# A stack of four graph layers on one Trainium2 core: the additive layer's layer norm and elu additions made by VectorE instead of GpSimd

## The chip, the cores and the metric

One Trainium2 chip, one of its cores. The metric is the device time of one execution in microseconds. A core has TensorE (PE, matrix products), VectorE (DVE), ScalarE (ACT), GpSimd (POOL) and SyncE (SP, which here only issues DMAs). They run side by side and wait for each other through semaphores.

## The reference

The input x holds 8 graphs of 1024 nodes with 64 features, adj one 1024x1024 mask per graph. Four layers follow one another, each after a layer norm with a relu, each added to x:

```python
h = jnp.maximum(_layernorm(x, axis=-1), 0.0)
x = x + _L0_gnn_ref(h, adj, ...)      # dot-product attention, one head
h = jnp.maximum(_layernorm(x, axis=-1), 0.0)
x = x + _L1_gnn_ref(h, adj, ...)      # dot-product attention, four heads
h = jnp.maximum(_layernorm(x, axis=-1), 0.0)
x = x + _L2_gnn_ref(h, adj, ...)      # additive attention: the layer of this change
h = jnp.maximum(_layernorm(x, axis=-1), 0.0)
x = x + _L3_gnn_ref(h, adj, ...)      # graph attention with a norm of its own
```

with

```python
def _layernorm(x, axis=-1, eps=1e-05):
    m = jnp.mean(x, axis=axis, keepdims=True)
    v = jnp.var(x, axis=axis, keepdims=True)
    return (x - m) / jnp.sqrt(v + eps)

def _L2_gnn_ref(h, adj, lin_w, lin_b, W_w, a):
    hp = jnp.einsum('bni,oi->bno', h, lin_w) + lin_b
    u = jnp.einsum('bnf,of->bno', hp, W1)
    v = jnp.einsum('bnf,of->bno', hp, W2)
    s = u[:, :, None, :] + v[:, None, :, :]
    s = jnp.where(s > 0, s, ALPHA * s)
    e = jnp.einsum('bijf,f->bij', s, a[:, 0])
    e = jnp.where(adj > 0, e, NEG_INF)
    attention = jax.nn.softmax(e, axis=2)
    h_prime = jnp.einsum('bij,bjf->bif', attention, hp)
    return jax.nn.elu(h_prime)
```

The costly part of the additive layer is s: for each graph 1024 x 1024 pairs of nodes by 64 features, each with its own kink before the sum over features.

## The kernel before, in words

x stays in SBUF for the whole program, as 128 partitions x 8 graphs x 8 blocks x 64 features. Each layer is a block of its own with one program per engine. The additive layer starts at some 1390 us of the span and ends at some 3380 us.

**Units.** The layer goes through 8 graphs (b) and, in each, 8 units (n) of 128 rows: 64 units. A unit's scores are the sum of 16 sets (positions k = 0 to 15). A set is 8 rows of the unit times 1024 columns, in four groups. Each set is made by one of two engines and summed by PE into a PSUM bank pair, one for even and one for odd units:
- DVE makes its sets in `make_set` (L1089), two instructions of 128x2048 f32 per set, called ring pieces below. They go to a ring of 4 sets, and DVE waits only if the set four back has not been summed.
- ACT makes 6 or 7 of the 16 sets of a unit (`SCALAR_SETS`, 7 in units 1 and 5), four instructions of 128x1024 per set (L975), into a ring of 3.
- PE takes the sets in the order of k, whoever made them (`sum_set`, L912 for ACT's and L922 for DVE's).

**What else stands in a unit.** Everything else is put at a fixed position k by hand. For the unit before: the masked maximum on DVE at k = 3 (L257, then negmax at L260), the exponential on ACT at 6 (L269), the turning of the rows on PE at 7 (L198), the two copies out of PSUM at 10 (L239, half on DVE and half on ACT), the product with the values on PE at 11 (L220), the division on DVE at 15 (L1143, L1145). For the next graph: nine fills, which are the small products that make its inputs. PE makes three in each of units 1, 2 and 3 at k = 3, 7 and 11, and DVE takes each out of PSUM three positions later (`take_fill`; L1008 takes fills 0 and 1, L1010 fills 2 and 3). The coding of the next graph's inputs into half-precision parts is on DVE in units 4 to 7 (L1025 to L1079). The last graph has no fills and no coding.

**The layer norm.** It is worked two graphs ahead, graph b making the normed rows of graph b + 2 (the last two graphs make those of graphs 0 and 1 for the next layer). DVE makes the mean in unit 4 at k = 4 (`layer_norm_mean`, L137 and L139). POOL then subtracts it and squares (`layer_norm_centre`, L148 and L151). DVE sums the squares and makes the variance in unit 6 at k = 6 (`layer_norm_scale`, L168 and L156). POOL then makes the inverse root (`inverse_root`, L161, on 8 numbers per partition) and multiplies by it (`layer_norm_apply`, L179). These POOL operations, but for the root, are 128x512 f32.

**The elu.** When a graph is done, in unit 1 of the next one, DVE makes min(z, 0) and max(z, 0) - 1 at k = 1 (`elu_parts`, L766 and L767), ACT makes the exponential of the former at its k = 4 (L773), and POOL adds the two (L874) and adds the sum to x (L876). After the last graph the same is done once more, with nothing beside it, and then the block ends and the next layer starts (its first DVE instruction is L1529).

Semaphores of the change: `mean_ready`, `square_ready`, `seed_ready` (the variance), `y_ready` (the normed rows), `elu_exp`, and `x_added`, which counts two per graph. DVE itself waits for `x_added` before it uses the elu's two tiles for coding (unit 5) and before the next `elu_parts`. PE waits for `y_ready` before the fills that turn the normed rows, `fill_ready` says that it has, and that tile may be overwritten.

Of the kernel before, what the change touches and what calls it, by code (L numbers as in the profile page):

```python
# [36 lines left out]
ALU = mybir.AluOpType  # L37
# [3 lines left out]
P = 128  # L41
# [9 lines left out]
STARTS = 1  # L51
# [3 lines left out]
def wait(eng, sem, value):  # L55

    if not isinstance(value, int) or value > 0:
        eng.wait_ge(sem, value)
# [67 lines left out]
def next_norm(s, b):  # L126

    return b + 2 - s.B if isinstance(b, int) and b + 2 >= s.B else b + 2
# [4 lines left out]
def layer_norm_mean(v, s, sems, b, done):  # L133

    nc = s.nc
    wait(v, sems["y_ready"], done)
    nc.vector.tensor_reduce(s.stat[:, 0, :], s.graph(b), AX.X, ALU.add)  # L137
    v.drain()
    nc.vector.tensor_scalar(s.stat[:, 1, :], s.stat[:, 0, :], 1.0 / s.D, None, ALU.mult).then_inc(sems["mean_ready"], 1)  # L139


def layer_norm_centre(g, s, sems, b, done):

    nc = s.nc
    shape = [P, s.NB, s.D]
    g.wait_ge(sems["mean_ready"], done + 1)
    wait(g, sems["y_ready"], done)
    nc.gpsimd.tensor_tensor(s.centred[:], s.graph(b), s.stat[:, 1, :].unsqueeze(2).to_broadcast(shape),  # L148
                            ALU.subtract).then_inc(sems["centred_ready"], 1)
    g.wait_ge(sems["centred_ready"], done + 1)  # L150
    nc.gpsimd.tensor_tensor(s.square[:], s.centred[:], s.centred[:], ALU.mult).then_inc(sems["square_ready"], 1)  # L151


def variance(v, s, stat, total):

    return s.nc.vector.tensor_scalar(stat[:, 3, :], total, 1.0 / s.D, LN_EPS, ALU.mult, ALU.add)  # L156


def inverse_root(g, s, stat, out):

    return s.nc.gpsimd.tensor_tensor(out, stat[:, 3, :], s.minus_half[:], ALU.pow)  # L161


def layer_norm_scale(v, s, sems, b, done):

    nc = s.nc
    v.wait_ge(sems["square_ready"], done + 1)
    nc.vector.tensor_reduce(s.stat[:, 2, :], s.square[:], AX.X, ALU.add)  # L168
    v.drain()
    variance(v, s, s.stat, s.stat[:, 2, :]).then_inc(sems["seed_ready"], 1)  # L170


def layer_norm_apply(g, s, sems, b, par, done, y_free):

    g.wait_ge(sems["seed_ready"], done + 1)
    inverse_root(g, s, s.stat, s.stat[:, 7, :])
    g.drain()
    wait(g, sems["fill_ready"], y_free)
    s.nc.gpsimd.tensor_tensor(s.y[:, par, :, :], s.centred[:],  # L179
                              s.stat[:, 7, :].unsqueeze(2).to_broadcast([P, s.NB, s.D]),  # L180
                              ALU.mult).then_inc(sems["y_ready"], 1)
# [596 lines left out]
def additive_layer(nc, s, lin_w, lin_b, W_w, a_w):  # L778
# [5 lines left out]
    B, N, D, NB = s.B, s.N, s.D, s.NB  # L784
    K = 9
# [6 lines left out]
    with ExitStack() as ctx:  # L792
        def sb(name, shape, dt):
            return ctx.enter_context(nc.sbuf_tensor(f"l2_{name}", shape, dt))

        sems = make_sems(nc, ctx, "l2", ["vector_sets", "scalar_sets", "vector_summed", "scalar_summed", "coded", "elu_parts", "elu_exp",
                                         "raw_turned", "x_added"])
        raw = sb("raw", [D, 3, D], F32)
        lwT = sb("lwT", [P, D], F32)
        w1 = sb("w1", [P, 2, D], F32)  # L800
# [17 lines left out]
        low, high = (s.mask[:, 2 + i, :].bitcast(F32).rearrange("p (j d) -> p j d", j=NB) for i in range(2))  # L818
# [49 lines left out]

        @block.gpsimd
        def _(g):  # L870
            def elu_add(b):

                g.wait_ge(sems["elu_exp"], b + 1)
                nc.gpsimd.tensor_tensor(high[:], high[:], low[:], ALU.add).then_inc(sems["x_added"], 1)  # L874
                g.wait_ge(sems["x_added"], STARTS + 2 * b + 1)
                nc.gpsimd.tensor_tensor(s.graph(b), s.graph(b), high[:], ALU.add).then_inc(sems["x_added"], 1)  # L876

            for b in range(B):
                layer_norm_centre(g, s, sems, next_norm(s, b), b + 2)
                layer_norm_apply(g, s, sems, next_norm(s, b), b % 2, b + 2, b * K + 2)  # L880
                elu_add(b)

        @block.tensor
        def _(pe):
# [117 lines left out]
        def _(v):  # L1002
# [91 lines left out]
            def run(b, par, n, u, buf, fills, before=True, encode=False):  # L1094
                first, count = fills
                for k in range(SETS):
                    if k not in ON_SCALAR[n]:
                        make_set(par, n, u, k)
                    if k in TAKE_AT and TAKE_AT[k] < count:
                        take_fill(b + 1, 1 - par, first + TAKE_AT[k])  # L1100
                    if n == 4 and k == 4:
                        layer_norm_mean(v, s, sems, next_norm(s, b), b + 2)
                    if n == 6 and k == 6:
                        layer_norm_scale(v, s, sems, next_norm(s, b), b + 2)
                    if encode and n == 4 and k in (7, 11):
                        extremes(0, k // 11, w[:, 1 - par, :])
                    if encode and n == 5 and k in (2, 4):
                        extremes(1, k // 4, r[:, 1 - par, :])
                    if encode and n == 5 and k == 7:
                        find_range(1 - par)  # L1110
                        wait(v, sems["x_added"], STARTS + 2 * b)
                    if encode and (n, k) in ((5, 11), (6, 11)):
                        code_half_w(1 - par, n - 5)
                    if encode and n == 7 and k == 4:
                        code_r(1 - par)
                    if encode and n == 7 and k == 11:
                        code_signs(1 - par)
                    if k == BATCH and n == 1 and b > 0:
                        batch_end(b - 1)
                    if not before:  # L1120
                        continue
                    if k == MAX:
                        logit(1 - buf, u - 1)
                    if k == COPY:
                        copy_half(v, nc.vector.tensor_copy, s, sems, 0, u - 1)
                    if k == FINISH:
                        finish((n - 1) % NB, 1 - buf, u - 1)

            def batch_end(b):
                v.drain()  # L1130
                wait(v, sems["x_added"], STARTS + 2 * b)
                elu_parts(v, s, sems, z[:], low, high)
# [8 lines left out]
            def finish(n, slot, u):  # L1141
                v.wait_ge(sems["out_ready"], u + 1)
                nc.vector.reciprocal(s.rinv[:, slot:slot + 1], unit_out[:, D:D + 1])  # L1143
                v.drain()
                nc.vector.tensor_scalar(z[:, bass.ds(n, 1), :].rearrange("p a d -> p (a d)"), unit_out[:, 0:D],  # L1145
                                        s.rinv[:, slot:slot + 1], None, ALU.mult).then_inc(sems["unit_done"], 1)
# [52 lines left out]
            copy_half(v, nc.vector.tensor_copy, s, sems, 0, u)  # L1199
            finish(NB - 1, 1, u)  # L1200
            batch_end(B - 1)

# [406 lines left out]
```

## Time and profile before

| | |
|---|---|
| median of 3 runs | 3784.64 us (3781.56 to 3786.26) |
| the profiled execution, its own time | 3785.15 us |
| span of the profiled execution | 3783.4 us |
| mean granted TensorE clock | 0.954 of full speed |
| busy, share of the span | PE 84%, DVE 86%, ACT 78%, POOL 27% |

Busy time of an engine is the time in which one of its instructions runs; waiting, semaphore and DMA-issuing instructions are left out. Instructions of one engine overlap a little, so a start-to-start step can be shorter than the duration shown. A line number is the line of the kernel, and where a helper makes an instruction, the helper's. The timeline merges neighbouring instructions of one kind: x4 means four of them, and the time is from the first's start to the last's end. In brackets stands the idle time of the engine before the row and what ended it.

### The profile page before, as it was taken

What the parts mean: (1) busy time and instruction counts of PE and PEld (TensorE: products, weight loads), DVE (VectorE), ACT (ScalarE), POOL (GpSimd) and SP (SyncE); (2) the same over time, 40 slices, a digit from 0 to 9 for tenths busy, and PEclk for the clock granted to TensorE, in tenths of its full rate; (3) what the DMA queues carried; (4) which work ended last, traced back from release to release, by engine and by line L of the source; (5) the groups of instructions that cost most, each with busy time, mean ns of one, the idle gap of its engine ahead of it and who ended that gap; (6) DMA issues with size and microseconds to landing.
All of it is one profiled execution on the core that took longest, in us unless ns stands there. A gap on an engine that the chain in (4) does not pass through costs nothing. (4 is left out here: it accounts for less than half of the span.)

```text
span 3783.4 us, 80082 instructions
## 1 busy us (share of the span) xinstructions
PE 3194.2 (84%) x31515; PEld 1745.3 (46%) x31515; DVE 3269.9 (86%) x5325; ACT 2960.2 (78%) x3529; POOL 1014.7 (27%) x565
## 2 busy tenths in 40 slices
PE   6886988998999878889898898888988978878786
PEld 4663666665666643333333333333333323336665
DVE  7885887887888779999999999999999999966666
ACT  4554877887788758989899899888998889956555
POOL 4332555555555630000000001000000000016554
PEclk9997999999999989999999999999999999988887
DMA  6551000000000000000000000000000000001111
GB/s 180 172 183 38 18 17 17 18 18 19 18 18 15 21 13 7 10 12 10 10 10 10 10 10 10 10 10 10 11 12 10 10 10 10 10 14 52 49 51 43
DMA packets 67260, 110.69 MB, mean 29 GB/s; under 512 B 25941, under 2 KB 25944, under 8 KB 66904
## 3 DMA queue, kind: packets, MB, share of 16 engines
q1 hardware_dynamic: 66904, 105.77, 9.4%
q8 instruction: 245, 4.01, 0.4%
q14 instruction: 111, 0.91, 0.1%
HBM read 86.87 MB, written 18.87 MB: 28 GB/s over the span
## 5 line engine op out<-in xcount | busy, mean ns | idle before, releaser
L975 ACT ACTIVATE l_scalar_ring<-l_w,l_r 128x1024 f32<-128x1024 f32 x1600 | 1679.8, 1143 | 35.7 <-DVE l_values L1021 26.1
L1089 DVE TENSOR_SCALAR l_vector_ring<-l_w_code,l_r_code 128x2048 f32<-128x2048 f32 x1248 | 1619.2, 1362 | 3.5 <-issue 0.2
L922 PE MATMUL scores<-l_vector_ring,l_signs_code 128*32 128x512 f16 x9984 | 686.4, 396 | 194.8 <-DVE l_vector_ring L1089 193.7
L912 PE MATMUL scores<-l_scalar_ring,l_signs 128*32 128x512 f32 x6400 | 781.3, 607 | 67.7 <-ACT l_scalar_ring L975 66.7
L239 ACT COPY probs_t<-turned 128x512 f32<-128x512 f32 x512 | 293.4, 586 | 494.7 <-PE turned L198 491.5
L434 POOL TENSOR_TENSOR l_masked<-l_relu,mask 128x1024 f32<-128x1024 f32 x256 | 545.5, 2131 | 493.8 <-ACT l_relu L582 491.2
L922 PEld LDWEIGHTS scores<-l_vector_ring,l_signs_code 128*32 128x32 bf16 x9984 | 240.0, 96 | 669.8 <-DVE l_vector_ring L1089 399.2
L209 PE MATMUL outT<-probs_t,l_values 128*64 128x128 f32 x6144 | 436.6, 285 | 66.0 <-ACT probs_t L239 26.3
L198 PE MATMUL turned<-ident,l_probs 128*128 128x128 f32 x3072 | 437.7, 288 | 11.4 <-issue 7.3
L209 PEld LDWEIGHTS outT<-probs_t,l_values 128*64 128x64 f32 x6144 | 345.1, 140 | 214.6 <-DVE l_acc L665 102.4
L269 ACT ACTIVATE l_probs<-l_logits,negmax,l_bound 128x1024 f32<-128x1024 f32 x320 | 397.6, 1242 | 6.8 <-DVE negmax L260 6.8
L912 PEld LDWEIGHTS scores<-l_scalar_ring,l_signs 128*32 128x32 f32 x6400 | 197.1, 111 | 442.8 <-issue 265.7
L257 DVE CUSTOM_DVE_ANT_0 l_logits<-scores,l_masked 128x1024 f32<-128x1024 f32 x256 | 313.4, 1224 | 98.5 <-POOL l_masked L434 62.8
L198 PEld LDWEIGHTS turned<-ident,l_probs 128*128 128x128 f32 x3072 | 348.4, 146 | 83.1 <-issue 69.9
L239 DVE COPY probs_t<-turned 128x512 f32<-128x512 f32 x384 | 263.4, 686 | 56.4 <-PE turned L198 51.8
L148 POOL TENSOR_TENSOR centred<-x_res,stat 128x512 f32<-128x512 f32 x32 | 41.5, 1298 | 889.7 <-DVE stat L139 889.5
L582 ACT ACTIVATE l_relu<-scores 128x1024 f32<-128x1024 f32 x256 | 260.2, 1016 | 6.5 <-PE scores L509 6.5
L508 PE MATMUL scores<-l_kh,l_q 128*128 128x512 f16 x640 | 246.6, 385 | 12.4 <-ACT l_values L567 5.0
L509 PE MATMUL scores<-l_kl,l_q 128*128 128x512 f16 x640 | 247.2, 386 | 0.0
L161 POOL TENSOR_TENSOR stat<-stat,minus_half 128x8 f32<-128x8 f32 x32 | 70.3, 2197 | 492.5 <-DVE stat L156 491.9
L231 PE MATMUL outT<-add_halves,turned_out 128*128 128x64 f32 x640 | 127.2, 280 | 81.1 <-DVE turned_out L246 80.5
L1290 POOL TENSOR_TENSOR l_base<-l_dst_slope,mask 128x1024 f32<-128x1024 f32 x64 | 144.2, 2257 | 120.7 <-DVE negmax L260 100.9
(244 smaller groups left out, 3331.8 us busy)
## 6 DMA issues: line engine op xcount, KB each, us to landing
mask<-masks_kept SPq DMA_DIRECT2D x192, 256.0 KB, 2.6
l_adj<-adj SPq DMA_DIRECT2D x64, 512.0 KB, 4.4
masks_kept<-mask SPq DMA_DIRECT2D x64, 256.0 KB, 2.3
x_res<-x SPq DMA_DIRECT2D x8, 256.0 KB, 5.0
out<-x_res SPq DMA_DIRECT2D x8, 256.0 KB, 3.5
l_w_both<-L_gnn_Wq SPq DMA_DIRECT2D x2, 64.0 KB
l_w_both<-L_gnn_Wk SPq DMA_DIRECT2D x2, 64.0 KB
l_w_both<-L_gnn_Wv SPq DMA_DIRECT2D x2, 64.0 KB
```

The lines of the kernel that those rows point to most:

```text
L198: last = s.nc.tensor.transpose(s.turned[:, j, :], probs[:, j * P:(j + 1) * P], s.ident[:])
L209: last = s.nc.tensor.matmul(s.outT[half * s.D:(half + 1) * s.D, 0:P], values[:, j, :], s.probs_t[:, j, :], start=(j < 2), stop=(j >= s.NB ...
L239: copy(s.probs_t[:, half * n:(half + 1) * n, :], s.turned[:, half * n:(half + 1) * n, :]).then_inc(sems[f"half{half}_copied"], 1)
L257: s.nc.vector.tensor_tensor_reduce(out=out, in0=logits, in1=mask, scale=1.0, scalar=-3e38, op0=ALU.add, op1=ALU.max, accum_out=s.rowmax[:, ...
L269: s.nc.scalar.activation(probs, logits, ACT.Exp, bias=s.negmax[:, slot:slot + 1], scale=scale, accum_out=total).then_inc(sems["probs_ready ...
L434: nc.gpsimd.tensor_tensor(masked[:, n % 2, :], relu4[:, n % 2, :], s.mask[:, i, :], ALU.add).then_inc(sems["masked_ready"], 1)
L509: last = nc.tensor.matmul(out, lhs, kl[:, par, h, cols], start=False, stop=True)
L582: nc.scalar.activation(relu4[:, n % 2, :], scores[n % 2], ACT.Relu, scale=1.0 / SLOPE - 1.0).then_inc(sems["relu_ready"], 1)
L912: last = nc.tensor.matmul(s.scores[g * ROWS:(g + 1) * ROWS, buf, half, :], signs[:, window], scalar_ring[:, at % SCALAR_RING, g, halves[ha ...
L922: last = nc.tensor.matmul(s.scores[g * ROWS:(g + 1) * ROWS, buf, half, :], signs_code[:, par, g % 2, window], parts(vector_ring[:, at % VE ...
L975: last = nc.scalar.activation(scalar_ring[:, at % SCALAR_RING, g, :], w[:, par, :], ACT.Relu, bias=r[:, par, column:column + 1])
L1089: last = nc.vector.tensor_scalar(vector_ring[:, at % VECTOR_RING, g:g + 2, :], w_code[:, par, :, :], r_code[:, par, 0, column:column + 1], ...
```

## The change

VectorE gets the five tensor-tensor operations per graph, and GpSimd keeps the inverse root. The centring and square are put in unit 4 at k = 9, the scaling in unit 6 at k = 14, and the elu's additions in unit 1 at k = 8, and after the last graph. Between two operations of one pair there is now a drain on DVE in place of a semaphore. The scaling waits for a new semaphore, `root_ready`.

```diff
         @block.gpsimd
         def _(g):
-            def elu_add(b):
-
-                g.wait_ge(sems["elu_exp"], b + 1)
-                nc.gpsimd.tensor_tensor(high[:], high[:], low[:], ALU.add).then_inc(sems["x_added"], 1)
-                g.wait_ge(sems["x_added"], STARTS + 2 * b + 1)
-                nc.gpsimd.tensor_tensor(s.graph(b), s.graph(b), high[:], ALU.add).then_inc(sems["x_added"], 1)
-
             for b in range(B):
-                layer_norm_centre(g, s, sems, next_norm(s, b), b + 2)
-                layer_norm_apply(g, s, sems, next_norm(s, b), b % 2, b + 2, b * K + 2)
-                elu_add(b)
+                g.wait_ge(sems["seed_ready"], b + 3)
+                inverse_root(g, s, s.stat, s.stat[:, 7, :]).then_inc(sems["root_ready"], 1)
...
                     if n == 4 and k == 4:
                         layer_norm_mean(v, s, sems, next_norm(s, b), b + 2)
+                    if n == 4 and k == 9:
+                        centre_rows(next_norm(s, b), b + 2)
                     if n == 6 and k == 6:
                         layer_norm_scale(v, s, sems, next_norm(s, b), b + 2)
+                    if n == 6 and k == 14:
+                        scale_rows(b, par)
+                    if n == 1 and k == 8 and b > 0:
+                        elu_add(b - 1)
...
+            def centre_rows(g, done):
+
+                shape = [P, NB, D]
+                v.wait_ge(sems["mean_ready"], done + 1)
+                nc.vector.tensor_tensor(s.centred[:], s.graph(g), s.stat[:, 1, :].unsqueeze(2).to_broadcast(shape), ALU.subtract)
+                v.drain()
+                nc.vector.tensor_tensor(s.square[:], s.centred[:], s.centred[:], ALU.mult).then_inc(sems["square_ready"], 1)
+
+            def scale_rows(b, par):
+
+                v.wait_ge(sems["root_ready"], b + 1)
+                v.wait_ge(sems["fill_ready"], b * K + 2)
+                nc.vector.tensor_tensor(s.y[:, par, :, :], s.centred[:], s.stat[:, 7, :].unsqueeze(2).to_broadcast([P, NB, D]),
+                                        ALU.mult).then_inc(sems["y_ready"], 1)
+
+            def elu_add(b):
+
+                v.wait_ge(sems["elu_exp"], b + 1)
+                nc.vector.tensor_tensor(high, high, low, ALU.add)
+                v.drain()
+                nc.vector.tensor_tensor(s.graph(b), s.graph(b), high, ALU.add).then_inc(sems["x_added"], 2)
...
             finish(NB - 1, 1, u)
             batch_end(B - 1)
+            elu_add(B - 1)
```

## Rows read from the trace of the kernel before

**Rows 1.** The page's busy times of the whole span: engine, us, share, instructions.

```profile
PE 3194.2 (84%) x31515; PEld 1745.3 (46%) x31515; DVE 3269.9 (86%) x5325; ACT 2960.2 (78%) x3529; POOL 1014.7 (27%) x565
```

**Rows 2.** Window: us; PE, PEld, DVE, ACT, POOL busy; clock; DMA share; GB/s.

```profile
1423.00:3363.00 1940.00, 1677.17 (x18432) 665.07 (x18436) 1894.30 (x1980) 1759.10 (x1721) 101.33 (x46) 0.98 0.03 10
```

**Rows 3.** Waits of DVE in that stretch: us in total, times, longest.

```profile
DVE l_hpT L1010 <- PE fill L893: 13.6, 7, 2.1
```

**Rows 4.** The ring pieces' line: duration in ns, least/median/most, first and last start.

```profile
L1089 DVE TENSOR_SCALAR l_vector_ring<-l_w_code,l_r_code x1248: 1325/1340/2379, 1423.2 to 3361.7; 128x2048 f32<-128x2048 f32 x179
...
L1089 DVE TENSOR_SCALAR l_vector_ring<-l_w_code,l_r_code 128x2048 f32<-128x2048 f32 x1248 | 1619.2, 1362 | 3.5 <-issue 0.2
```

**Rows 5.** Timeline of POOL in one graph: start, us, instruction, idle before.

```profile
2101.79 3.73 POOL L161 TENSOR_TENSOR stat<-stat,minus_half 128x8 f32<-128x8 f32 x1 [61.24 <-DVE stat L156]
2105.66 1.97 POOL L179 TENSOR_TENSOR y<-centred,stat 128x512 f32<-128x512 f32 x1
2186.73 1.29 POOL L874 TENSOR_TENSOR mask<-mask 128x512 f32<-128x512 f32 x1 [79.10 <-ACT mask L773]
2188.10 2.14 POOL L876 TENSOR_TENSOR x_res<-x_res,mask 128x512 f32<-128x512 f32 x1
2281.15 2.07 POOL L148 TENSOR_TENSOR centred<-x_res,stat 128x512 f32<-128x512 f32 x1 [90.90 <-DVE stat L139]
```

**Rows 6.** Timeline of DVE: ring pieces over those, undisturbed, and a graph later.

```profile
2101.62 8.35 DVE L1089 TENSOR_SCALAR l_vector_ring<-l_w_code,l_r_code 128x2048 f32<-128x2048 f32 x6
...
2106.65 2.07 DVE L1089 TENSOR_SCALAR l_vector_ring<-l_w_code,l_r_code 128x2048 f32<-128x2048 f32 x1
...
2187.34 6.50 DVE L1089 TENSOR_SCALAR l_vector_ring<-l_w_code,l_r_code 128x2048 f32<-128x2048 f32 x4
...
2194.36 5.10 DVE L1089 TENSOR_SCALAR l_vector_ring<-l_w_code,l_r_code 128x2048 f32<-128x2048 f32 x4
...
2280.98 6.56 DVE L1089 TENSOR_SCALAR l_vector_ring<-l_w_code,l_r_code 128x2048 f32<-128x2048 f32 x4
...
2432.36 7.03 DVE L1089 TENSOR_SCALAR l_vector_ring<-l_w_code,l_r_code 128x2048 f32<-128x2048 f32 x4
```

**Rows 7.** DVE tensor-tensor work in the last layer: one line's durations, and a timeline.

```profile
L1490 DVE TENSOR_TENSOR l_work<-l_work,l_gamma x8: 681/940/2240, 3489.1 to 3778.1; 128x512 f32<-128x512 f32 x8
...
3557.96 0.68 DVE L1473 TENSOR_TENSOR l_work<-l_high,l_low 128x512 f32<-128x512 f32 x1
3558.71 0.69 DVE L1475 TENSOR_REDUCE l_total<-l_work 128x8 f32<-128x512 f32 x1
```

**Rows 8.** Timelines of PE and DVE in unit 1, up to the fill.

```profile
2196.08 1.92 PE L912 MATMUL scores<-l_scalar_ring,l_signs 128*32 128x512 f32 x16 [0.96 <-ACT l_scalar_ring L975]
...
2198.95 1.09 PE L198 MATMUL turned<-ident,l_logits 128*128 128x128 f32 x8
...
2199.39 0.67 DVE L1008 TENSOR_SCALAR hT<-fill 64x512 f32<-64x512 f32 x1
...
2207.85 0.68 DVE L1010 COPY l_hpT<-fill 64x512 f32<-64x512 f32 x1 [2.05 <-PE fill L893]
```

**Rows 9.** Unit 1 a graph later: PE, DVE; a window (columns of rows 2).

```profile
2436.93 1.81 PE L922 MATMUL scores<-l_vector_ring,l_signs_code 128*32 128x512 f16 x16 [1.85 <-DVE l_vector_ring L1089]
...
2446.09 0.69 DVE L239 COPY probs_t<-turned 128x512 f32<-128x512 f32 x1 [0.34 <-PE turned L198]
...
2437.00:2441.00 4.00, 4.00 (x32) 1.27 (x36) 4.00 (x4) 4.00 (x5) 0.00 (x0) 0.57 0.00 0
```

**Rows 10.** Timelines of the last graph (unit 5) and of the layer's end.

```profile
3297.63 0.69 DVE L239 COPY probs_t<-turned 128x512 f32<-128x512 f32 x1 [4.21 <-PE turned L198]
...
3376.14 0.63 ACT L773 ACTIVATE mask<-mask 128x512 f32<-128x512 f32 x1 [5.65 <-DVE mask L767]
...
3378.18 1.26 POOL L876 TENSOR_TENSOR x_res<-x_res,mask 128x512 f32<-128x512 f32 x1
...
3379.83 0.11 DVE L1529 MEMSET l_w<- 64x64 f32 x1 [3.73 <-PEq L792]
```

More of the change, by code:

```diff
@@ L796, in additive_layer @@
         sems = make_sems(nc, ctx, "l2", ["vector_sets", "scalar_sets", "vector_summed", "scalar_summed", "coded", "elu_parts", "elu_exp",
-                                         "raw_turned", "x_added"])
+                                         "raw_turned", "x_added", "root_ready"])
         raw = sb("raw", [D, 3, D], F32)
```

## The prediction, made before the changed kernel was run

> **What bounds the kernel now.** I read the page first: VectorE (DVE) is busy for 86% of the span, TensorE (PE) for 84%, ScalarE (ACT) for 78%, GpSimd (POOL) for 27% [rows 1]. That is an average over four layers, and the change touches one, so I cut out its main stretch by windows, from the first to the last piece that DVE makes for the ring: 1940 us in which DVE is busy for 1894 us (98%), ACT for 91%, PE for 86% and POOL for 5% [rows 2]. The waits of DVE in that stretch hold only one regular item, 2.05 us once per graph, 13.6 us in seven waits [rows 3]. So each microsecond of DVE work is a microsecond of the layer, except where DVE stands just before such a wait.
>
> Next, what POOL's work does to DVE. The main instruction, the ring piece at L1089, took 1340 ns at the median, 1362 ns in the mean and 2379 ns at most over 1248 pieces [rows 4]: some of them are stretched. The timelines of POOL and DVE side by side show which. In one graph POOL makes six instructions, of which [rows 5] hold five; the square comes right behind the centring. An undisturbed run of four ring pieces takes 5.10 us. The four pieces that lie over POOL's centring and square take 6.56, which is 1.46 more. The six over the root and the scaling take 8.35, where six undisturbed ones would take 5.10 + 2 x 1.255 = 7.61, which is 0.74 more. The four over the two additions of the elu take 6.50, which is 1.40 more, and one graph later 7.03, 1.93 more [rows 6]. POOL loses too: its second addition took 2.14 us there and 1.26 us at the layer's end, where DVE does nothing [rows 5, 10]. The root by itself (3.73 us on POOL) stretches nothing: the extra 0.74 lies in the one piece of 2.07 us that begins at 2106.65, under the scaling [rows 6].
>
> A rule of the Trainium skill is stricter than these rows. Its page "SBUF — State Buffer", section "SBUF: two separate sides", says that the port pair shared by VectorE and GpSimd is an exclusive lock, held for a whole instruction, while the other engine fully blocks. The rows show 0.7 us of delay per POOL tensor operation, less than the 1.26 us that an addition takes undisturbed, so in my sum the rows decide; what the rule would make of it is rival C.
>
> **The change, part by part.**
> Taken away: five POOL tensor operations per graph, and with them the stretch of DVE's pieces. Over the layer that is 8 x 1.46 = 11.7 us for centring and square, 8 x 0.74 = 5.9 us for the scaling, and for the elu (seven times inside the loop, three times at about 1.4 and four at about 1.9) 11.8 us. Together 29.4 us. As a check, the mean less the median over all pieces gives 0.022 x 1248 = 27.5 us [rows 4].
> Added: five tensor-tensor operations of 128x512 f32 on DVE per graph. The same form with two plain SBUF inputs took 0.68 us at L1473 [rows 7]. Started back to back, instructions cost about 0.08 us less than their duration (four of 1.34 in 5.10), so 0.60 us; with a drain behind it the step from one start to the next is 0.75 us [rows 7]. Centring and square: 0.75 + 0.60 = 1.35 us. Scaling: 0.60. Two additions: 1.35. No trace row has a DVE operation with an input repeated along the row. I bound it from below by 0.68 us (L1473) and from above by the longest of L1490, which has one repeated along the other axis: 681 ns least, 940 median, 2240 most [rows 7]. I take 0.68, since the least of L1490 equals it and its long ones lie beside POOL's work of the last layer.
> Not on the path: the new waits. DVE reaches position 14 of unit 6 eight positions after it gave POOL the variance. Five of these are its own sets of two pieces, so at least 5 x 2 x 1.255 = 12.5 us pass, while the root takes 3.73 us; if the root were late by x, all ring pieces behind it would be late by x. ACT's exponential of the elu is done at its position 4, DVE asks for it at position 8. The mean is DVE's own. No DMA is moved, and POOL's queue holds nothing else that anyone waits for.
>
> Now what of each pair reaches the end.
> *Centring and square* (unit 4): 1.46 - 1.35 = 0.11 us gained per graph, in a DVE-bound stretch. Seven graphs: 0.8 us. In the eighth, DVE waits 4.21 us for the turned rows one unit later [rows 10], which swallows it.
> *Scaling* (unit 6): 0.74 - 0.60 = 0.14 us, eight graphs, 1.1 us.
> *Elu* (unit 1): on DVE's own account 11.8 - 7 x 1.35 = 2.4 us. But here ACT sets the pace: PE waited 0.96 us for an ACT piece just before it turned the rows, DVE ended the piece of work ahead of the copy at 2200.06, the turn was done at 2200.04, and DVE then waited 2.05 us for the fill behind the next ACT piece [rows 8]. A shorter DVE path makes that wait longer. What can come back is a side effect in the later graphs: the stretched piece starves PE for 1.85 us, the granted clock of the four microseconds behind is 0.57 (part of it at 1.2 instead of 2.4 GHz), and both DVE and ACT then wait 0.35 us for the turned rows [rows 9]. With no such stretch this goes: 3 graphs x 0.35 = 1.0 us (the fourth, the last graph, has its 4.21 us wait behind it).
> *The layer's end*: ACT's exponential ends at 3376.77; POOL's additions end at 3379.44 and the next layer starts at 3379.83 [rows 10]. On DVE the two end 0.75 + 0.68 us after the exponential, at 3378.2: 1.2 us gained, with nothing to hide it.
>
> **Sum:** 0.8 + 1.1 + 1.0 + 1.2 = 4.1 us less. The profiled execution took 3785.15 us (3783.4 of span and 1.75 around it), so 3781.0; the median of the three runs is 0.5 below the profiled one, so I forecast **3780.5 us**, 0.11% less. About 0.2% (7.6 us) is what a measurement of this kernel can tell from no change, so this counts as the same.
>
> **Rivals.**
> A. *DVE's account counts everywhere.* If ACT's hold on unit 1 gives way when DVE's path shortens, all of it counts: 29.4 removed, 8 x 1.35 + 8 x 0.60 + 7 x 1.35 = 25.1 added, 1.2 at the end: 5.5 us less, 3779.1. For it: DVE is busy 98%. Against: the 2.05 us wait. Still the same within 0.2%. Chance 0.14.
> B. *Slower: the tensor-tensor operations cost DVE much more than 0.68 us.* Place: units 4 and 6, where DVE has no wait to cover them, 8 x 3 operations. At 1.3 us, between the median and the longest of L1490 [rows 7], each costs 0.62 more: 14.9 - 4.1 = 10.8 us slower, 3795.4. It decides from 7.6 + 4.1 = 11.7 us over 24 operations, that is from 1.17 us each. For it: L1490 reached 2240 ns, and the inputs are read with a repeated column. Against: it reached that beside POOL instructions, while here POOL has only the root, done before the scaling starts. Chance 0.07. The same section of the Trainium skill's page says that a VectorE operation with two SBUF inputs waits only for a GpSimd operation that reads SBUF; by it, too, the root would be the only thing to meet.
> C. *Faster: the stretch removed is larger than the ring pieces show.* If each POOL operation held DVE for all of its undisturbed time (1.26 us for an addition, which I take for all five as an upper end), 38 operations would have cost 47.9 us against 25.1 added: 24.0 us less with the end, 3760.6. The lock rule of the Trainium skill's page gives this. Against: 6.50 less 5.10 is 1.40 for two operations, not 2.5. Chance 0.03, and 0.03 more for something between this and my sum that passes 7.6 us, such as clock dips worth more than 1.0 us.
> D. *Nothing counts but the end.* If ACT or PE also paces units 4 and 6, only the 1.2 us at the end remains: 3783.4. Same. Chance 0.12.
>
> **Chances and range.** Forecast 0.61, A 0.14, D 0.12, B 0.07, C with its neighbours 0.06. Faster by over 0.2%: 0.06. Slower: B, 0.07. Same: 0.87. The range takes in A and D, the spread of the runs shown (2.5 us to either side) and 0.1 us more or less on each of the 38 operations, half of it covered: 3776 to 3787.
>
> **What the changed profile would show.** POOL busy in the stretch of [rows 2] falls from 101 us to some 30, only the roots. L1089's mean falls to its median of 1340 ns, with a maximum under 1400. Five new DVE groups of 128x512 f32, eight each, means of 680 ns. The once-per-graph wait of DVE stays near 2 us or grows by some tenths. PE has no wait of 1.5 to 1.9 us at unit 1, and the clock keeps its level there in the later graphs. The stretch itself is 2 to 4 us shorter. I would be wrong if the new groups were above 1 us, if L1089 kept stretched pieces, or if DVE showed a wait for the root.

## The result and the profile after

The changed kernel takes 3774.55 us (median of 20 runs, 3768.2 to 3783.18) against 3782.54 us for the kernel before on the same chips. The ratio is 0.998, 95% interval 0.9973 to 0.9987: 8 us faster, where 4.1 were forecast (3780.5 us). The time lies 1.5 us below the stated range of 3776 to 3787. Of the 6 us between forecast and median, 2.1 come from the base: the forecast started from the median of three runs, 3784.64 us, and twenty gave 3782.54. With the ratio applied to the forecast's own base the time would be 3777.1 us, just inside the range. The gain itself is about twice the forecast. What was forecast inside the additive layer did not come as forecast, and most of the gain is made in another layer, by something that the forecast did not look at.

| us, from one profile each | before | after |
|---|---|---|
| span | 3783.4 | 3774.2 |
| from the start to the first ring piece | 1423.2 | 1421.0 |
| additive layer: first ring piece to the next layer's first DVE instruction | 1956.6 | 1956.1 |
| last layer | 403.5 | 397.1 |

The layer that was changed is as long as it was; the layer behind it is 6.4 us shorter. I took these times from the starts of the first ring piece and of the last layer's first memset in each trace.

First the page of the changed kernel, to be read against [rows 1] and [rows 4]:

```profile
PE 3184.7 (84%) x31515; PEld 1738.5 (46%) x31515; DVE 3268.1 (87%) x5365; ACT 2961.7 (78%) x3529; POOL 943.0 (25%) x525
...
L1081 DVE TENSOR_SCALAR l_vector_ring<-l_w_code,l_r_code 128x2048 f32<-128x2048 f32 x1248 | 1591.9, 1340 | 3.4 <-issue 0.2
```

The ring pieces have lost their stretch: 1619.2 us of busy time have become 1591.9, and the mean is 1340 ns, the former median. That is 27.3 us removed, where the prediction's sum had 29.4 and its check 27.5. The groups of DVE that are new, over the layer's main stretch (by line and form: busy us, mean ns):

```profile
L1133 DVE TENSOR_TENSOR square<-centred 128x512 f32<-128x512 f32 x8 | 5.5, 693 | 0.6
L1139 DVE TENSOR_TENSOR y<-centred,stat 128x512 f32<-128x512 f32 x8 | 5.5, 682 | 0.0
L1131 DVE TENSOR_TENSOR centred<-x_res,stat 128x512 f32<-128x512 f32 x8 | 5.4, 680 | 0.0
...
L1147 DVE TENSOR_TENSOR x_res<-x_res,mask 128x512 f32<-128x512 f32 x7 | 4.8, 692 | 0.5
L1145 DVE TENSOR_TENSOR mask<-mask 128x512 f32<-128x512 f32 x7 | 4.7, 677 | 0.0
```

All five cost what the forecast took, 0.68 us. An input repeated along the row costs nothing extra (680 and 682 ns against 693 for the square, which has none). Now the waits of DVE in the same stretch, which answer to [rows 3] (us in total, times, longest):

```profile
DVE l_hpT L1002 <- PE fill L885: 13.6, 7, 2.1
DVE hT L1000 <- PE fill L187: 4.3, 5, 1.3
DVE probs_t L239 <- PE turned L198: 3.6, 9, 0.8
DVE rinv L1163 <- PE outT L220: 2.9, 2, 1.5
```

The 2.05 us wait per graph is unchanged. The second line is new: 4.3 us in five waits for a fill, at position 10 of unit 1. The timelines of DVE, PE and ACT around one of them (the first two rows are the additions themselves):

```profile
2194.91 0.68 DVE L1145 TENSOR_TENSOR mask<-mask 128x512 f32<-128x512 f32 x1
2195.66 0.69 DVE L1147 TENSOR_TENSOR x_res<-x_res,mask 128x512 f32<-128x512 f32 x1
...
2200.13 0.68 DVE L1000 TENSOR_SCALAR hT<-fill 64x512 f32<-64x512 f32 x1 [1.26 <-PE fill L187]
2201.15 0.69 DVE L239 COPY probs_t<-turned 128x512 f32<-128x512 f32 x1 [0.34 <-PE turned L198]
...
2195.51 3.29 PE L904 MATMUL scores<-l_scalar_ring,l_signs 128*32 128x512 f32 x16 [2.38 <-ACT l_scalar_ring L967]
...
2201.15 0.59 ACT L239 COPY probs_t<-turned 128x512 f32<-128x512 f32 x1 [1.54 <-PE turned L198]
```

and the window of the four microseconds behind PE's gap (columns of [rows 2]):

```profile
2196.00:2200.00 4.00, 4.00 (x24) 1.55 (x16) 2.87 (x3) 3.61 (x4) 0.00 (x0) 0.58 0.02 6
```

Compare [rows 8]. There PE had lost time to the stretched pieces first:

```profile
2191.38 1.12 PE L922 MATMUL scores<-l_vector_ring,l_signs_code 128*32 128x512 f16 x16 [1.45 <-DVE l_vector_ring L1089]
```

and then waited 0.96 us for ACT's piece, and the granted clock of 2196 to 2200 us was 1.00. Here DVE's pieces come on time, so PE runs through them and waits 2.38 us for the same piece of ACT in one gap. Behind the gap the granted clock is 0.58 (part of the four microseconds at 1.2 GHz), the 16 products take 3.29 us instead of 1.92, and the turned rows come late for DVE and for ACT. The stretch on DVE has become a gap on PE. The gap of 2.4 us stands in all seven graphs, but a low clock stands behind it in three of them only (at 1704, 2195 and 2687 us: 0.57, 0.61 and 0.57 over four microseconds; at 1951, 2442, 2934 and 3180 us it is 1.00). In those three DVE waits 1.3 us for the fill. In the kernel before the same place had a low clock in four graphs of the seven (0.57 to 0.59), where DVE then waited 0.3 to 0.7 us for the turned rows [rows 9]. So the low stretches of this place have not become more, but each holds DVE for longer.

The end of the layer, against [rows 10]:

```profile
3374.64 0.63 ACT L773 ACTIVATE mask<-mask 128x512 f32<-128x512 f32 x1 [5.29 <-DVE mask L767]
...
3376.07 0.69 DVE L1147 TENSOR_TENSOR x_res<-x_res,mask 128x512 f32<-128x512 f32 x1
3377.12 0.11 DVE L1550 MEMSET l_w<- 64x64 f32 x1 [0.36 <-PEq L792]
```

From the end of the exponential (3375.27) to the next layer it is now 1.85 us; it was 3.06 (3376.77 to 3379.83). The 1.2 us of the forecast are there.

Two signs that the forecast named did not come. The stretch from the first ring piece to the last was to be 2 to 4 us shorter; it is 1939.1 us against 1938.5. And PE was to have no long wait in unit 1, with its clock kept.

What is left is the last layer. Its waits of DVE that no other engine ends ("issue"), first in the kernel before:

```profile
DVE l_z L1465 <- issue: 3.0, 1, 3.0
DVE rinv L1462 <- issue: 2.7, 1, 2.7
DVE x_res L1494 <- issue: 1.4, 4, 0.5
```

and after the change:

```profile
DVE x_res L1515 <- issue: 0.7, 4, 0.2
...
DVE rinv L1483 <- issue: 0.2, 1, 0.2
```

Two idle times of DVE, 5.7 us together, have gone but for 0.2 us, in a layer of which not one line was changed. They stand once in the program's run, close behind the additions to x of the second graph (3539.43) in a loop that holds two graphs per turn. In the 30 us around that place the trace of the kernel before has five packets of DMA traffic of the kind "instruction" on this queue:

```profile
q14 instruction: 5, 0.04, 0.4%
```

and, after the change:

```profile
q14 instruction: 1, 0.01, 0.1%
```

The other profiles of the case divide in the same way: all six with the stall (the kernel before and, of the experiments below, e1, e4, e5, e10 and e14) have five such packets there, and those without it have one, but for e3, which has three.

### The profile page after: what moved, and what is told of

Read it like the earlier page. It is cut to its first block and busy times, and to the rows that moved or that the text cites. A ratio compares the mean times of both kernels' runs of the same rounds, so it can differ in the third digit from the quotient of the medians.

```text
span 3774.2 us, 80090 instructions
## 1 busy us (share of the span) xinstructions
PE 3184.7 (84%) x31515; PEld 1738.5 (46%) x31515; DVE 3268.1 (87%) x5365; ACT 2961.7 (78%) x3529; POOL 943.0 (25%) x525
## 5 line engine op out<-in xcount | busy, mean ns | idle before, releaser
L1081 DVE TENSOR_SCALAR l_vector_ring<-l_w_code,l_r_code 128x2048 f32<-128x2048 f32 x1248 | 1591.9, 1340 | 3.4 <-issue 0.2
L257 DVE CUSTOM_DVE_ANT_0 l_logits<-scores,mask 128x1024 f32<-128x1024 f32 x128 | 156.1, 1219 | 6.2 <-PE scores L509 3.0
```

The source lines that it names most:

```text
L257: s.nc.vector.tensor_tensor_reduce(out=out, in0=logits, in1=mask, scale=1.0, scalar=-3e38, op0=ALU.add, op1=ALU.max, accum_out=s.rowmax[:, ...
L1081: last = nc.vector.tensor_scalar(vector_ring[:, at % VECTOR_RING, g:g + 2, :], w_code[:, par, :, :], r_code[:, par, 0, column:column + 1], ...
```

## The experiments

Theory 1 is the forecast's sum. Theory 2: the last layer's time follows from how and when the additive layer ends. Theory 3: in unit 1, the elu's additions on DVE cost clock through PE's gap. Theory 4, formed after the second series: the change makes DVE's program longer, so the code of the last layer's loop lies elsewhere, and a stall for code goes. Every ratio below is to the kernel before, with its 95% interval. "Additive layer" is always from the first ring piece to the next layer's first DVE instruction.

### The same kernel again, and the parts alone

`e1_before_again` is the kernel before, unchanged. `e2_norm_only` leaves the elu on POOL, `e3_elu_only` the norm, `e4_end_only` everything but the two additions after the last graph. The cuts show GpSimd's program, e2 against the changed kernel, e3 and e4 against the kernel before:

```diff
 e2:             for b in range(B):
                     g.wait_ge(sems["seed_ready"], b + 3)
                     inverse_root(g, s, s.stat, s.stat[:, 7, :]).then_inc(sems["root_ready"], 1)
+                    elu_add(b)
 e3:             for b in range(B):
                     layer_norm_centre(g, s, sems, next_norm(s, b), b + 2)
                     layer_norm_apply(g, s, sems, next_norm(s, b), b % 2, b + 2, b * K + 2)
-                    elu_add(b)
 e4:
-                    elu_add(b)
+                    if b < B - 1:
+                        elu_add(b)
```

> The kernel before, unchanged, run as if it were a change: it tells how far two series of the same kernel lie apart and how far two profiles of it differ in each layer. The additive layer's stretch, from DVE's first ring piece to its last, was 1938.5 us before and 1939.1 us after; the last layer, from its first DVE instruction to the end, 403.5 and 397.1. Theory 1 (the gain is made in the additive layer, as in the forecast's sum): this profile repeats 1938.5 within 1 us, and the last layer swings by several us without meaning. Theory 2 (the gain is made in the last layer, which starts from another state after the change): the last layer is again 403 to 404 us. Ratio 1.000 within 0.001 by both.

> Only the norm's centring, square and scaling on DVE; the elu's additions stay on POOL. Theory 1: removed 11.7 + 5.9, added 8 x 1.95 = 15.6, so 2 us less, ratio 0.9995; the ring pieces keep 11.8 us of stretch, all in unit 1. Theory 2 (the last layer gives the gain): nothing in the additive layer, and the last layer as in the kernel before, 403 us, since POOL still ends the additive layer; if it is 397 again, the cause in the last layer is not the elu at the end.

> Only the elu's additions on DVE, those after the last graph too; the norm stays on POOL. Theory 1: 1 us at unit 1 and 1.2 us at the end, ratio 0.9994; DVE's own account alone (rival A) would give 2.4 + 1.2 = 3.6 us, 0.999. Graph periods without the swing between 244.8 and 246.7 that the changed kernel shows would speak for the norm as its cause; with it, for the elu.

> Only the two additions after the last graph on DVE, everything else as before. Theory 1: 1.2 us less, ratio 0.9997. Theory 2 (the last layer's clock and stalls depend on how the additive layer ends): the last layer falls by up to 6 us with it, ratio 0.998, as for the whole change.

| | ratio (interval) | additive layer | last layer |
|---|---|---|---|
| e1, before again | 1.0009 (0.9999 to 1.0018) | 1958.9 | 396.5 |
| e2, norm only | 0.9982 (0.9974 to 0.9991) | 1950.3 | 395.5 |
| e3, elu only | 0.9989 (0.9979 to 0.9999) | 1958.3 | 401.8 |
| e4, end only | 0.9998 (0.9985 to 1.0011) | 1952.6 | 404.0 |

Four things follow. The last layer of one and the same kernel was 403.5 us in one profile and 396.5 in another, with the two stalls in both: a single profile can't price 6 us there. Theory 2 falls, since e4 begins the last layer as the changed kernel does and has neither its last layer nor its ratio. The norm alone gives as much as the whole change, three times theory 1's 2 us (part of this is the stall, as shown below). And the elu alone, whose additive layer is not shorter than before, still has 0.9989. The waits without a releaser, which I then compared over all profiles, split the kernels in another way: e1 has 3.2 + 2.6 us, e4 one of 6.1, e2 and e3 none.

### More work on POOL, more on DVE, other places for the elu

`e5_dup_pool` does POOL's centring, square and scaling twice, `e6_dup_dve` those on DVE. `e7_elu_at_5` and, later, `e12_elu_at_4` move the elu's additions, and `e8_norm_end` is e2 with the end on DVE. The cuts are against the changed kernel:

```diff
 e6, centring (the scaling likewise):
+                nc.vector.tensor_tensor(s.square[:], s.graph(g), s.stat[:, 1, :].unsqueeze(2).to_broadcast(shape), ALU.subtract)
+                v.drain()
+                nc.vector.tensor_tensor(s.centred[:], s.square[:], s.square[:], ALU.mult)
+                v.drain()
 e7:
-                    if n == 1 and k == 8 and b > 0:
+                    if n == 1 and k == 5 and b > 0:
 e12:
+                    if n == 1 and k == 4 and b > 0:
```

> The kernel before, with POOL's centring, square and scaling each done twice in the additive layer (24 POOL operations more). It prices what one POOL tensor operation takes from DVE. Theory 1 (each stretches DVE's ring pieces by 0.73 us and that is all): 17.5 us more, ratio 1.0046. Theory 2 (the stretch also starves PE, whose clock falls, and DVE waits for PE later): more than that, 20 to 30 us, with waits of DVE for the turned rows growing beyond the 5.9 us of before. If the stretch were largely hidden: under 10 us.

> The changed kernel, with the centring, square and scaling on DVE each done twice (24 DVE operations with drains more, 0.75 us each). Theory 1: 18 us more than the changed kernel, so ratio to the kernel before 0.998 + 0.0048 = 1.0028. If DVE's additions are partly hidden: clearly less, under 1.001. If bunching them starves PE and costs clock: over 1.004.

> The changed kernel with the elu's additions in unit 1 moved from position 8 to position 5, where POOL's stretch had been. Theory 3 (at position 8 they leave PE without a piece of ACT's for 2.4 us in one gap, its clock falls, the turned rows come 1 us late and DVE waits; at position 5 the gap splits in two, as with the stretch): DVE's waits for the fill at position 10 (4.3 us in the changed kernel) go, graph periods come down from 245.1 to 246.7 towards 244.6, and the stretch is 4 to 6 us shorter, ratio 0.9970. Theory 1 (the place doesn't matter, unit 1 follows ACT): 0.998 as the changed kernel.

> The norm's operations on DVE, the elu's additions in the loop on POOL, those after the last graph on DVE. Theory 1: e2's time less the 1.2 us at the end, ratio 0.9979. Theory 3 (elu in the loop on POOL does no harm): graph periods of 244.5 to 245.2 as in e2, the additive stretch 1932 us as in e2, faster than the changed kernel's profile by 5 us or more there.

> The changed kernel with the elu's additions in unit 1 at position 4, one earlier than e7 had them. Theory 3 (the earlier DVE makes them, the more the gap that PE has before ACT's piece of position 7 is split): the wait of DVE at the fill of position 10 goes from 4.3 us (position 8) and 1.5 (position 5) to nearly none, the additive layer with its end (1956.1 us in the changed kernel, 1952.5 in e7) falls to 1950 to 1952, ratio 0.9970 to 0.9980. If position 8 was only bad luck of the clock in e11 and the changed kernel: anything from 1952 to 1957, with that wait at any size. The last layer without the stall, as the program is as long as the changed kernel's.

| | ratio (interval) | additive layer | DVE's waits for the fill at position 10 |
|---|---|---|---|
| e5, POOL twice | 1.0024 (1.0011 to 1.0037) | 1965.1 | none |
| e6, DVE twice | 1.0015 (1.0006 to 1.0023) | 1970.1 | 4.7 |
| e7, elu at 5 | 0.998 (0.9971 to 0.9988) | 1952.5 | 1.5 |
| e12, elu at 4 | 0.9979 (0.997 to 0.9988) | 1954.7 | 3.4 |
| e8, norm and end | 0.9987 (0.9976 to 0.9998) | 1952.2 | none |

e6 adds 24 operations to the changed kernel, and the layer grows by 1970.1 - 1956.1 = 14.0 us, 0.58 each, where DVE's own account says 0.75. By the ratios it is 0.0035 x 3782 = 13 us. So about a quarter of what is put on DVE seems to fall into waits that it has anyway: its four waits for PE listed above go from 24.4 us in the changed kernel to 21.9 (13.5 + 4.7 + 2.1 + 1.6), 2.5 of the missing 4 us. e5 adds 24 operations on POOL, and the layer grows by 8.5 us where theory 1 said 17.5. Its timelines of POOL and DVE show why:

```profile
2284.61 2.07 POOL L882 TENSOR_TENSOR centred<-x_res,stat 128x512 f32<-128x512 f32 x1 [90.94 <-DVE stat L139]
2286.82 1.84 POOL L885 TENSOR_TENSOR square<-centred 128x512 f32<-128x512 f32 x1
2288.86 1.78 POOL L148 TENSOR_TENSOR centred<-x_res,stat 128x512 f32<-128x512 f32 x1 [0.20 <-issue]
2290.72 1.90 POOL L151 TENSOR_TENSOR square<-centred 128x512 f32<-128x512 f32 x1
...
2284.44 7.29 DVE L1106 TENSOR_SCALAR l_vector_ring<-l_w_code,l_r_code 128x2048 f32<-128x2048 f32 x4
2291.64 1.21 DVE L1042 TENSOR_REDUCE l_rng<-l_w 128x1 f32<-128x1024 f32 x1
```

The four ring pieces are stretched by 7.29 - 5.10 = 2.19 us, 0.73 for each of three POOL operations, as in [rows 6]. The fourth POOL operation lies over a reduction, and that took its usual 1.21 us. The price is paid by the ring pieces, not by whatever DVE does. Over the layer the busy time of the ring pieces grows from 1619.2 to 1630.2 us, 11.0 us or 0.46 per added operation. The rest of the difference to 8.5 us is in the waits: those for the turned rows fall from 5.9 to 1.7 us, those for the reciprocal (`rinv`) rise from 1.5 to 3.0.

Theory 3 is not borne out as a rule for where to put the additions. e7 has less of the wait and a shorter layer, but e12, one position earlier, has 3.4 us of it again, and the two ratios can't be told apart. The expectation of 0.997 for e7 was not met. The second profile of the changed kernel, e11, has 4.6 us of the wait and an additive layer of 1956.3 us, as the first. Only with the additions on POOL is the wait gone altogether.

e8 was expected at 0.9979 and came at 0.9987, slower than e2, though it differs from e2 only in the end, which the profiles show to be 1.2 us shorter. Differences of one or two microseconds between single series are not to be read.

### The place of the code

The number of DVE's instructions in the trace ahead of the last layer is 6911 in the kernel before and 6975 in the changed one. `e9_before_pad` gives the kernel before 64 drains more, in places where DVE waits; `e13_before_pad_again` is the same once more. `e10_after_pad` and `e14_after_pad_again` give the changed kernel 192 more, so that it has 256 more than the kernel before when it reaches the last layer's loop; 76 of them stand ahead of the second layer's weights, 40 at the end of the additive layer, 76 before the last layer's weights. `e11_after_again` is the changed kernel.

```diff
 e9, before the last layer's weights arrive (and as many at the end of the additive layer):
             nc.vector.memset(whT[D:P, :], 0.0).then_inc(sems["weights_ready"], 1)
+            for _ in range(32):
+                v.drain()
```

> The kernel before, with 64 drains more on DVE ahead of the last layer's loop, where DVE waits anyway (32 at the end of the additive layer, 32 before the last layer's weights arrive). DVE's program is then as long up to that loop as in the changed kernel, which has 64 instructions more. Theory 4 (part of the gain is that DVE's stall of 3.0 + 2.7 us without a releaser at the loop's end, which the kernel before and e1, e4 and e5 show and the changed kernel and e2, e3, e6, e7, e8 don't, has gone with the code's place): the two idle times 'issue' at the reciprocal and z go, ratio 0.9985 to 0.999. Theory 1 and 3 (all of the gain is made in the additive layer): the stall may go, but the time stays, 1.000 within 0.0007.

> The changed kernel with 192 drains more on DVE at three places where it waits (76 before the weights of the second layer, 40 after the last elu_parts, 76 before the weights of the last layer), so that its program has 256 instructions more than that of before up to the last layer. Theory 4, if a stall depends on the code's place in steps of 256 instructions: the stall of 5.7 us is back at the same two lines, ratio 0.9990 to 0.9995 where the changed kernel has 0.998. Theories 1 and 3: no stall, or none that costs; the time stays at 0.998, up to 0.999 for what the drains themselves may cost.

> The changed kernel once more: a second profile of it and a second comparison. Ratio 0.998 within 0.001. Theory 3 (unit 1 with the additions at position 8 costs clock): graph periods swing again between 244.8 and 246.7 and DVE waits at the fill at position 10; theory 4: the last layer is again without the stall. The last layer between 395.5 and 398 us, as in all kernels so far whose norm is on DVE.

> e9 once more, the kernel before with 64 drains. Theory 4 (the place of DVE's code decides the last layer's stall, and that is most of the gain): 0.9985 within 0.0007, no idle time of 2 us or more without a releaser on DVE, additive layer with its end 1956 us as before. If e9 was a lucky series: 1.000.

> e10 once more, the changed kernel with 192 drains. Theory 4: 0.9990 to 1.0000, the stall of 2.8 + 2.9 us at the reciprocal and z again. If the additive layer carried the gain: 0.998 to 0.9985. Its difference from e13 or from the kernel before is what the change is worth with the code in the same place: theory 1 says 4 us, the profiles of the additive layer so far say 1 us.

> e2 once more, only the norm on DVE. The additive layer with its end was 1950.3 us there and 1952.2 in e8, against 1952.6 to 1958.9 in the kernels with the norm on POOL. If that difference is real: again 1949 to 1953 and a ratio of 0.9975 to 0.9982; if it is the scatter of the clock: up to 1957.

DVE's waits without a releaser in the last layer, in e9:

```profile
DVE x_res L1496 <- issue: 0.7, 4, 0.2
...
DVE rinv L1464 <- issue: 0.2, 1, 0.2
```

and in e10:

```profile
DVE l_z L1490 <- issue: 2.9, 1, 2.9
DVE rinv L1487 <- issue: 2.8, 1, 2.8
DVE x_res L1519 <- issue: 1.4, 4, 0.5
```

The drains alone take the stall out of the kernel before, and 192 drains bring it back into the changed kernel, at the same two instructions (in e14 3.1 + 2.7 us). With it come the times. The means are over the single runs of a kernel (one run of the kernel before, 6946.62 us, is far off and left out; e3 had one of 8883.57 us), in brackets their number and the standard error; for the kernel before they are its runs beside all series but its own, e1:

| mean us | stall in the last layer | no stall |
|---|---|---|
| as before | 3781.5 (164, 0.4) | 3777.4 (e9, e13: 24, 0.7) |
| changed | 3779.2 (e10, e14: 24, 0.9) | 3774.9 (changed, e11: 32, 0.6) |
| norm only | | 3773.3 (e2, e15: 24, 0.5) |

Down a column stands what the change is worth with the code in the same place: 2.3 us with the stall, 2.5 without. Along a row stands what the stall costs: 4.1 and 4.3 us. Each of these four differences has a standard error of 0.8 to 1.1 us, and that is rather too small: e9 and e13, the same kernel, have means of 3775.8 and 3778.9. The row of the kernel before is the cleaner one, since its drains stand behind the additive layer; in e10 and e14 those ahead of the second layer's weights may change something there too (the first ring piece starts at 1416.1 and 1417.0 us, against 1417.0 to 1424.5 in the other profiles).

The ratios of the single series say the same less sharply: e9 0.9985 (0.9974 to 0.9996) and e13 0.9995 (0.9986 to 1.0004), e10 0.9996 (0.9986 to 1.0007) and e14 0.9999 (0.999 to 1.0008), e11 0.9984 (0.9974 to 0.9994), e15 0.9978 (0.9969 to 0.9988). e13 was expected within 0.0007 of 0.9985 and missed that. The additive layer is 1956.7 us in both e9 and e13, as in the kernel before, so their gain isn't made there.

Theory 4 holds: the stall follows the number of DVE instructions ahead of the loop in every kernel. With 0 or 3 (e4) more than in the kernel before it is there, with 24 (e3), 40 (e2, e15), 43 (e8), 64 and 112 (e6) more it isn't, with 256 more it is. That also gives a reason for e3's 0.9989 without a shorter additive layer.

The Trainium skill has a mechanism that fits, on its page "Runtime: NRT & Kernel Launch", section "Instruction fetch mechanics": each engine's code is brought in blocks of 256 instructions, ahead of need as long as the code runs straight on, and a taken branch to code that is not there has to wait for it. The trace agrees in both points that can be seen here. The stall stands in a loop, with five packets of instruction traffic around it where the kernels without it have one (e3 three), and it comes back when the program has been made 256 instructions longer (one such step was tried). Which block is missing at which branch no run here shows.

## Why the prediction was right or wrong

**Right: what POOL takes from DVE, and what DVE needs instead.** 27.3 us of stretch went (29.4 said), the five operations cost 0.68 us each, the root stretches nothing. In the changed kernel DVE never waits for the root. The price of 0.73 us per POOL operation in e5 speaks against rival C, that DVE is held for the whole undisturbed time of each: 3760 was never near. Rival B is out too: no new operation took over 0.70 us. Rival D, that only the end counts, is out by e2 and e15, which leave the end on POOL and are 4.1 us faster in the mean than e9 and e13, with no stall in any of the four.

**Right: the end.** 1.2 us said, 1.2 found.

**Wrong: the sum had no term for the code's place.** The step that failed is the cut to the additive layer alone: the sum prices the rest of the program at nothing, and the only sentence near it is that no DMA is moved. That holds for the kernel's own transfers and not for its instructions. The change lengthens DVE's program by 64 instructions, and that takes a stall out of the last layer's loop, worth 4.1 to 4.3 us. The means are 3781.5 - 3774.9 = 6.6 us apart (the ratio's interval allows 4.9 to 10.2 us), of which some 4.2 are the stall and 2.4 the change itself. The missing term is thus larger than the 2.5 us between forecast and means, and the terms that the forecast did have were together too large. The rows were there: 2.7 and 3.0 us of DVE idle with nothing that ends them is a thing to explain before the program around it is made longer.

**Wrong in size, both ways: the parts in the layer.** Centring, square and scaling were to bring 0.8 + 1.1 = 1.9 us. The profiles with the norm alone on DVE have an additive layer of 1950.3, 1952.2 and 1953.4 us, against 1952.6 to 1958.9 (mean 1956.3) for the five that leave it on POOL with the elu: about 4 us. The means without a stall say the same, 3777.4 - 3773.3 = 4.1 us. DVE's waits for the turned rows fall from 5.9 us to 1.4 in e2, those for the reciprocal rise from 1.5 to 2.6. The prediction took the 4.21 us wait of the last graph [rows 10] for a cushion that would swallow the gain there. That one wait is 3.5 to 4.3 us in all six profiles with the norm once on POOL and 0.6 us or none in all ten with it on DVE, so a good part of the norm's gain seems to be made just where the forecast put nothing. Why it goes is not shown: e5, with the norm twice on POOL, has only 1.1 us of it.

The elu was to bring 1.0 us in unit 1. No such gain is seen, but a loss isn't shown either. By the profiles the additive layer is some 3 us longer with the loop's additions on DVE (mean 1955.3 of six against 1952.0 of three), and e2 and e15 are 1.6 us faster in the mean than the changed kernel (3773.3 against 3774.9, standard errors 0.5 and 0.6). Against that, e8, which differs from the changed kernel in these additions alone, has a mean of 3775.9 us (standard error 0.9), slower by 1.0. The reasoning that ACT paces unit 1 was right. Its consequence was drawn only for DVE's wait; that PE would then stand idle in one gap, and that DVE would wait 1.3 us wherever the clock is low behind it, was missed, though [rows 9] show the same thing on a smaller scale for the stretched piece.

Together the change itself is worth 2.4 us with the code in the same place (standard error about 0.7), where 4.1 was said and rival A had 5.5. How it splits between norm, elu and end stays open: the single series and profiles that would tell scatter by about 3 us.

**The range** was too narrow because every one of its cases lay inside one layer, and because it was laid around a base of three runs; 164 runs of the kernel before have a mean of 3781.5 us, 3.1 below it.

No version tried is clearly better than the changed kernel. e2 and e15 (norm alone on DVE) have the lowest mean, by 1.6 us.

## What to carry to other kernels

An engine's program is a stretch of code with a place. Where a kernel has loops, look for idle times with no releaser before and after every edit that adds or removes instructions ahead of them, and when a gain or a loss appears in a part that was not changed, pad the old kernel to the new length before believing anything else. Work on POOL beside a DVE that is the bound cost DVE 0.7 us per 128x512 operation under the ring pieces here, about what DVE needs for doing it itself, so such a move was worth little either way. An engine freed of a stall hands the gap on to the next one in the chain: ask who then waits, and for how long in one piece.

## What was not expected of the hardware

- A program made longer by 64 instructions, or by 64 drains that do nothing, ran 4 us faster, and made longer by 256 it had lost that again: stalls of 2.7 + 3.0 us on DVE in a loop of the last layer.
- POOL's 128x512 operations stretch DVE's 128x2048 pieces (in f32, one tensor input) by 0.73 us each; a DVE reduction under the same POOL operation kept its 1.21 us, and the root of 3.7 us on POOL, on 8 numbers per partition, stretched nothing.
- The same gap of 2.4 us on PE, once per graph, was followed by a granted clock of 0.57 to 0.61 over four microseconds in three graphs of seven and by 1.00 in the other four.
- The last layer of one kernel, unchanged, took 403.5 and 396.5 us in two profiles, with a granted clock of 0.80 and 0.83 in it. Effects of a few microseconds need the means of dozens of runs.
